# Padding in front of an expert kernel's float32r buffers, so that they begin on multiples of 512 bytes

## What is computed

```python
xn = _layernorm(x, axis=-1)
# recurrence: B_x = xn @ B_w.T + B_b ; h_t = sigmoid(log_A) * h_{t-1} + B_x_t ; s = h @ C_w.T + C_b
s = _L0_attn_ref(xn, log_A, B_w, B_b, C_w, C_b)
# experts: top 2 of logits = xn @ Wr + br, softmax over the two;
#   gate = xn @ W1[e], up = xn @ W3[e], y = (silu(gate) * up) @ W2[e], weighted and summed
g = _silu(_L0_ffn_ref(xn, Wr, br, W1, W3, W2))
out = x + s * g
```

## Time and profile before

| | |
|---|---|
| median of the runs | 794.39 us |
| span of the profiled execution | 792.8 us, no own time is given beside it |
| TensorE (PE) busy | 767.7 us, 97% |
| VectorE (DVE), ScalarE (ACT), GpSimd (POOL) busy | 518.6, 375.8, 469.7 us |
| TensorE's share of the chain that ended last | 85% |
| bytes from and to HBM | 66.6 and 43.5 MB |

### The profile page before, as it was taken

One profiled execution on the slowest core, in us unless ns is written; L12 is line 12 of the kernel. 1 busy time (PEld: TensorE's weight loads), 2 busy tenths in 40 slices (PEclk: granted clock), 3 DMA queues, 4 the chain that ended last, 5 costly groups with the idle time before them and its releaser, 6 DMA issues.

```text
span 792.8 us, 17127 instructions
## 1 busy us (share of the span) xinstructions
PE 767.7 (97%) x5399; PEld 686.8 (87%) x5399; DVE 518.6 (65%) x1083; ACT 375.8 (47%) x666; POOL 469.7 (59%) x477
## 2 busy tenths in 40 slices
PE   4999989999999999999999999999999999999897
PEld 2554459999999999999998999999999999998786
DVE  6988976775778657666865664455556764552676
ACT  3975234544455435445644554445445654342430
POOL 4743847887577667846883586477547856454000
PEclk9999999999999999999999999999999999999999
DMA  9999912544555454425643644263537554952995
GB/s 287 347 308 322 134 53 97 134 74 96 124 117 115 95 112 84 69 49 138 140 74 87 167 67 73 41 140 67 113 68 192 100 127 90 320 90 34 290 370 195
DMA packets 101842, 111.02 MB, mean 140 GB/s; under 512 B 15634, under 2 KB 89236, under 8 KB 101748
## 3 DMA queue, kind: packets, MB, share of 16 engines
q0 software_dynamic: 25920, 35.54, 27.2%
q1 hardware_dynamic: 50032, 50.34, 20.0%
q10 hardware_dynamic: 25796, 24.20, 10.4%
HBM read 66.61 MB, written 43.45 MB: 139 GB/s over the span
## 4 chain that ended last, share of the span: by engine, by line
PE 85%; DVE 5%; ACT 4%; DMA 3%; issue 2%; POOL 1%; ACTq 0%; DVEq 0%; POOLq 0%; SPq 0%
PE bank L1507 15%; PE bank L1506 15%; PE bank L1508 15%; PE bank L1532 15%; PE bank L1533 7%; PE bank L1639 5%; PE bank L1495 3%; PE bank L1407 3%; DVE xnT L1085 2%; ACT xnT L666 1%; ACT h_sb L688 1%; PE bank L1558 1%; PE bank L1559 1%; PE bank L1557 1%; PE bank L1635 1%
## 5 line engine op out<-in xcount | busy, mean ns | idle before, releaser
L607 POOL DMA_INDIRECT y_rows<-y_sb,token_at x128 | 214.9, 1679 | 141.0 <-DVE y_sb L1203 73.5
L1506 PE MATMUL bank<-xh,W_sb 128*128 128x256 f32 x1008 | 283.1, 281 | 0.1
L1507 PE MATMUL bank<-xh,W_sb 128*128 128x256 f32 x1008 | 281.7, 279 | 0.0
L1508 PE MATMUL bank<-xl,W_sb 128*128 128x256 f32 x1008 | 281.6, 279 | 0.0
L1506 PEld LDWEIGHTS bank<-xh,W_sb 128*128 128x128 f32 x1008 | 189.2, 188 | 2.3 <-DVE xl L1151 0.4
L1532 PE MATMUL bank<-W_sb,hh 128*128 128x512 f32 x512 | 188.9, 408 | 1.3 <-DVE y_sb L1203 1.3
L1507 PEld LDWEIGHTS bank<-xh,W_sb 128*128 128x128 f32 x1008 | 189.4, 188 | 0.0
L1508 PEld LDWEIGHTS bank<-xl,W_sb 128*128 128x128 f32 x1008 | 188.9, 187 | 0.0
L1191 DVE TENSOR_TENSOR hbuf<-hbuf,bank 128x512 f32<-128x512 f32 x128 | 87.4, 686 | 153.8 <-PE bank L1508 149.4
L598 POOL DMA_INDIRECT xg<-xn_rows,token_at x128 | 144.7, 1131 | 38.3 <-POOL token_at L594 18.5
L1533 PE MATMUL bank<-W_sb,hl 128*128 128x256 f32 x512 | 143.8, 281 | 0.0
(11 more groups left out here) (254 smaller groups left out, 940.9 us busy)
## 6 DMA issues: line engine op xcount, KB each, us to landing
x_late<-L_attn_x SPq DMA_DIRECT2D x24, 512.0 KB, 10.0
raw<-L_ffn_W ACTq DMA_DIRECT2D x24, 512.0 KB, 4.0
odd_raw<-L_ffn_W ACTq DMA_DIRECT2D x21, 512.0 KB, 5.4
xn_rows<-h_sb SPq DMA_DIRECT2D x16, 512.0 KB, 6.4
y_rows<-xnT SPq DMA_DIRECT2D x4, 2048.0 KB, 15.9
yy<-y_rows SPq DMA_DIRECT2D x16, 512.0 KB, 9.0
out<-x_late SPq DMA_DIRECT2D x11, 512.0 KB, 7.3
x_kept<-L_attn_x SPq DMA_DIRECT2D x4, 512.0 KB, 6.7
```

What stands on the lines that cost most here:

```text
L607: return eng.indirect_dma_start(out=y_rows, out_offset=rows, in_=y, in_offset=None, bounds_check=T + TW - 1, oob_is_err=True, compute_op=A ...
L1506: eng.matmul(part, high, x_h, start=k == 0, stop=False)
L1507: eng.matmul(part, low, x_h, start=False, stop=False)
L1508: last = eng.matmul(part, high, x_l, start=False, stop=k == KD - 1)
```

## The change

Two tensors are added that nothing reads or writes. `to_line` has 24 float32 (96 bytes) in each partition behind `Bb_sb`, which moves everything that is allocated after it; `xg_to_line` has 112 float32 (448 bytes) behind `xg`, whose 8,256 bytes are not a multiple of 512. Both are deleted as Python names at once.

```diff
         A_sb = sb("A_sb", [P, KN], f32)
         Bb_sb = sb("Bb_sb", [P, KN], f32)
+        to_line = sb("to_line", [P, 24], f32)
...
             W_sb = sb("W_sb", [P, 2 * W_COLS], f32r, mid)
             xg = sb("xg", [P, XG_RING, 2, ROW], f32, mid)
+            xg_to_line = sb("xg_to_line", [P, 112], f32, mid)
             xh = sb("xh", [P, KD * TW], f32r, mid)
...
-        del pad_to_weights, odd_weights
+        del pad_to_weights, odd_weights, to_line, xg_to_line
```

## The result

The changed kernel takes 799.39 us (median of 4 runs, 798.63 to 800.98) against 794.96 us for the kernel before in the same comparison (4 runs, 794.36 to 796.14). The ratio is 1.0056, with a 95% interval of 1.0037 to 1.0074. It is slower by half a per cent; the forecast was 2.7% faster.

What follows compares the result with a forecast made beforehand. TensorE's matmul rate was taken as the bound (busy 97% of the span). -22.5 + 1 = -21.5 us, 0.5 given back: -21, so 792.8 becomes 771.8, with the median 1.6 above, 773 us; range 752 to 805.

Steps and rivals of the forecast that it cites:

- The bound: Expert part: TensorE is busy for 100.00 of 100.00 us, so only its matmuls' own rate can change the time.
- The three rates: Float32r matmuls of 256 columns: 120.0 ns in first tile and odd pieces, usually 117.8, 113.3 right behind the first tile's.
- all operands before lie 32 bytes past a multiple of 64: Expert part's float32r matmuls: whole 64-byte lines after the change bring 113.3 ns, 22.5 us saved less 1 us.
- equal rests: Expert part: weights and moving columns at the same rest run at 120.0 ns; +10 us, 804.4 us; chance 0.27.
- 2.2 ns x 4,560 units: Gate, up and down: usual float32r matmuls at the worst rate seen, 120.0 ns, cost 10 us.
- no effect: Float32r matmuls: the rates come from SBUF region, PSUM bank or phase, which padding leaves unchanged; 794 us; chance 0.24.
- the 753 that got 0.18: Float32r matmuls: the case that all of the loss goes, 753 us; chance 0.18.
- 4.5 ns x 4,560: Gate, up and down: usual matmuls go to 113.3 ns; with 6.7 x 300 for the others, 22.5 us saved.
- Other engines: ScalarE, VectorE and GpSimd in the expert part: 28 to 50 us of slack in 100, so changed rates cost nothing.
- the DMAs: Loads and stores of moved buffers: 0, plus or minus 1 us for the head, where loads of 10 us feed the chain.

Runs made afterwards that it cites:

- e2: Rows-only kernel: the kernel before plus 448 bytes in front of xh, nothing in front of the weights; 801.59 us.
- e5: Kernel before with 192 bytes in front of xh and 256 in front of odd_xh, gate and up at distance 256; gate and up 120.0 ns, no total given.
- e1: Front-only kernel: the kernel before plus the 96 bytes in front, none behind xg, and 64 in front of odd_xh; 793.15 us against 793.97.
- e6: Kernel before with 128 bytes in front of xh, 192 of hh, 192 of odd_xh; gate and up 113.4 ns in two tiles of three, no total given.
- e12: Kernel before with 128 bytes in front of xh and 480 in front of odd_xh; 786.97 us against 794.58, ratio 0.9898.
- e15: Kernel before with 128 bytes in front of xh, 160 of hh, 320 of odd_xh; 784.52 us against 795.85, ratio 0.985.
- e16: Layout of e12 with 160 bytes more in front, W_sb at rest 64 and xh, xl at 256; expert part 602.6 us against 603.4.
- e11: Changed kernel with only 64 of 128 weight columns in gate and up; gate and up 113.3 ns, no total given.
- e13: Changed kernel with only 32 of 128 weight columns in gate and up; 113.3 ns in 43 tiles, 117.8 in 17, no total given.

## Why the prediction was wrong

**The bound, right.** TensorE's rate of float32r matmuls is all that the change could touch in the expert part, and is what it touched: no new wait there (0.7 us in place of 1.3), full windows (100.00 of 100.00 us), same granted clock (1.00).

**The three rates, read rightly, the cause not.** All three came back: 120.0 in the changed kernel, e2 and e5, 117.8 in e1, 113.4 in e6, e12, e15 and e16, with others (116.7, 118.7) beside them. The step that failed is "all operands before lie 32 bytes past a multiple of 64, so each 64 bytes that TensorE reads touch two 64-byte lines ... After the change the lines are whole". No run shows that TensorE reads in lines of 64 bytes; they were an assumption of mine. The front-only kernel has the operands of gate and up on multiples of 64 and runs them at the old rate (117.8), the rows-only kernel has them 32 past one at the new rate (120.0), and e16 has them on multiples of 64 and at the good distance, without going under 113.3. Alignment to 64 bytes made no difference to gate and up's rate in any of them; the distance between the standing and the moving operand did, from 113.4 to 120.0 ns. The mistake behind it was to hold 113.3 and 120.0 ns for two prices per bytes read; they are two of several steady rates, and the distance has a say in which of them a tile runs at.

**The rival "equal rests" had the right quantity.** It was in the rows: the first tile and the odd pieces of gate and up have equal rests, and nothing else ran at 120.0. I held two things against it. The first was that the loss is as large in matmuls of 512 columns, which have one weight load where the same columns of gate and up have two. That is a wrong reading. The only matmuls of 512 columns with equal rests were those of the odd tiles' down, and they were not at 120.0. In the kernel before, three pairs from one L1574 to another:

```profile
196.63 0.28 PE L1574 MATMUL bank<-odd_W,odd_hl 128*128 128x256 f32 x1
...
197.69 0.28 PE L1574 MATMUL bank<-odd_W,odd_hl 128*128 128x256 f32 x1
```

1.06 us, 353 ns a pair, no more than down at 64 apart. The second was that the 113.3 at the earlier trace rows has the same rests as the usual 117.8. That is true, and only says that one distance can have two locks.

**Its size was off.** Forecast +10 us to 804.4; measured +4.4. The term was 2.2 ns x 4,560 units of 256 columns. Gate and up, 3,024 units, paid their part: +6.6 us. Down's 1,536 paid nothing, -0.7 us (360 ns a pair expected, 348 to 353 measured), as the two rows above could have told: with 353 ns for down at distance 0 the rival's sum is 2.2 x 3,024 = +6.7 us. The one wait of the earlier trace rows and the restart behind it shrank by 0.7, and about 1 us was saved outside the expert part, for part of which the last section has a likely source. 6.6 - 0.7 - 0.1 - 0.7 = 5.1 for the expert part, less 1.1 is the 4.1 by which the span grew (the terms are rounded).

**The rival "no effect"** fell with gate and up's rate, which went from 117.8 to 120.0 ns with the addresses alone.

**The rates under 113.3 rest on an estimate.** The lower end of the range, 752, and the 753 that got 0.18 had a float32r matmul of 256 columns at 109 ns, about half of plain float32's 216. No run shows a float32r matmul at that rate, nor at the 107, 109 and 110 that some expectations name: no tile in any run was steadily under 113.3. The forecast's own 4.5 ns x 4,560 is the step from 117.8 to 113.3, which both stand in the rows; the change made it +2.2 ns on gate and up.

**Other engines and head: 0, right.** Plain float32 kept its rate: eight matmuls of 256 columns take 1.73 us in the tail after the change as before, the head's twenty of 512 columns 8.64. For the DMAs I had taken 0, plus or minus 1 us; head and tail together gave 1.1 us, 0.9 of it in the tail, where I had expected nothing. "A difference of rest shows nothing there", said of the stores, doesn't hold for the loads of yy (last section).

**What stays open.** What repeats every 256 bytes, why a distance has two locks and what decides which one a tile falls into, and what holds the best steady rate at 113.3 ns. Fewer weight columns, other distances and starts on multiples of 64 gave none below it. Where the weights that are loaded and the columns that move get in each other's way, and whether they do, was not shown.

## What to carry to other kernels

When float32r matmuls of 256 columns run back to back and stand clearly more than 113.3 ns apart (the best steady rate here, at a granted clock of 1.00), look at the difference between the addresses of the standing and the moving operand modulo 256 bytes: 0 was the worst for these here (120.0 ns), 192 the best (113.4), and between them the rate followed no simple curve, so a distance has to be measured. Two pads, 128 bytes in front of xh and 480 in front of odd_xh, were worth 1.0%, nearly all of it by the first. Aligning all buffers to the same multiple of 256 bytes or more makes this difference 0; the changed kernel did so and ran gate and up at 120.0. If instructions of one kind show several steady rates in a trace, make a table of everything in which they differ before you give the loss a cause, give most weight to the difference that fits the most places, even if it lacks a mechanism, and look up the rate of every place that it names: the odd tiles' down was one, and it had the size of the loss in it.

## What the runs showed that I had not expected

**Two locks for one distance.** The same matmuls on the same addresses ran at 117.8 or at 113.3 ns from tile to tile in one execution, each without a break for up to 48 matmuls.

**Some large DMAs landed sooner from a start on a multiple of 512 bytes.** Issues of the changed kernel, to be held against the earlier trace rows:

```profile
x_late<-L_attn_x SPq DMA_DIRECT2D x24, 512.0 KB, 9.6
yy<-y_rows SPq DMA_DIRECT2D x16, 512.0 KB, 8.2
out<-x_late SPq DMA_DIRECT2D x11, 512.0 KB, 6.4
out<-x_kept SPq DMA_DIRECT2D x4, 512.0 KB, 7.7
```

The loads of yy are the clear case: 8.1 to 8.2 us in the four kernels where yy begins at rest 0 (the changed one, e1, e11, e13), 9.0 to 9.3 in the fourteen others, with rest 416 or, in e16, 64. Stores from x_late took 6.4 us in the changed and the front-only kernel (4.7 and 4.8 in e11 and e13) and 6.6 to 7.4 in all kernels with rest 416 or 64, a spread that leaves me unsure of the stores. Of the loads into x_late nothing can be read: kernels with rest 416 had anything from 8.8 (e6) to 10.0 us. And it isn't a gain everywhere: three loads of `raw` took 12.9 us in the changed kernel and 13.3 in the front-only one, against 9.7 before. Stores from x_kept, never moved, stayed at 7.6 to 7.9.

Little of this shows in the time: from the last down to the end 65.9 us before, 65.0 after and 65.2 in the front-only kernel. Behind the last down TensorE waits for the last add and then for a load of yy. In the chain that ended last that add took 3.82 us before and 3.54 after, that load 4.12 and 3.85, which is 0.55 of the 0.9 us. Whether the new addresses did that is not shown; single executions differ by as much in the tail.
